# A recurrent attention stage: the written order of its 2208 steps replaced by a rule, with filler matmuls before some waits

## The reference

```python
def step(S, inp):                      # one token, per head of 64
    rt, dt, kt, vt, at, bt = inp
    sa = einsum('bhij,bhj->bhi', S, at)
    S = S * dt[:, :, None, :] + sa[..., None] * bt[:, :, None, :] + vt[..., None] * kt[:, :, None, :]
    y = einsum('bhij,bhj->bhi', S, rt)
...
r, w, k, v, g, a = ...                 # projections of mixtures of x and the token before
y = wkv7(r, w, k, v, -kk, kk * a)      # the scan over 256 tokens
...                                    # group norm, bonus term, gate, output projection
```

## Time and profile before

| | |
|---|---|
| median of 3 executions | 3634.73 us (3626.49 to 3639.4) |
| profiled execution, its own time | 3626.49 us |
| its span, first to last instruction | 3624.7 us |
| busy: PE, DVE, ACT, POOL | 83%, 70%, 50%, 29% of the span |
| mean granted clock of TensorE | 0.893 of full speed |
| stage C | about 1767 to 3189 us of the span |

### The profile page before, as it was taken

One profiled execution on the slowest core, in us unless ns is written; L12 is line 12 of the kernel. 1 busy time (PEld: TensorE's weight loads), 2 busy tenths in 40 slices (PEclk: granted clock), 3 DMA queues, 4 the chain that ended last, 5 costly groups with the idle time before them and its releaser, 6 DMA issues.

```text
span 3624.7 us, 117284 instructions
## 1 busy us (share of the span) xinstructions
PE 3004.9 (83%) x51666; PEld 1961.9 (54%) x51666; DVE 2534.7 (70%) x5294; ACT 1821.0 (50%) x3063; POOL 1048.0 (29%) x1164
## 2 busy tenths in 40 slices
PE   6989999998648988988578888888888887679995
PEld 4555555555325555555245555555555555458773
DVE  3666666665548888988467777877777776457774
ACT  3334444443437888787244544444444552246661
POOL 0332222212431111212232332333333332045552
PEclk8889989989769999999778989989988886689997
DMA  2227999300043344430200000000000000056666
GB/s 75 79 97 290 395 394 327 35 1 1 32 138 125 128 134 138 143 135 21 70 3 4 12 10 11 11 11 11 10 10 10 10 11 14 9 189 227 224 214 180
DMA packets 161676, 356.89 MB, mean 98 GB/s; under 512 B 13821, under 2 KB 98559, under 8 KB 154896
## 3 DMA queue, kind: packets, MB, share of 16 engines
q1 hardware_dynamic: 147088, 323.95, 26.4%
q0 software_dynamic: 14080, 25.45, 2.1%
HBM read 136.33 MB, written 216.67 MB: 97 GB/s over the span
## 4 chain that ended last, share of the span: by engine, by line
PE 45%; issue 19%; DVE 12%; ACT 10%; SPq 9%; DMA 2%; POOL 1%; another core or an unknown queue 0%; DVEq 0%; POOLq 0%; ACTq 0%
PE ps L1551 8%; SPq L2548 8%; PE ps L135 3%; PE ps L137 3%; PE ps L136 3%; PE ps L1616 3%; PE ps L896 2%; ACT t L1035 2%; ACT t L1033 2%; PE ps L903 2%; PE ps L1658 1%; PE ps L875 1%; DVE t L1229 1%; PE ps L1628 1%; ACT t L1037 1%
## 5 line engine op out<-in xcount | busy, mean ns | idle before, releaser
L1551 PE MATMUL ps<-t 128*128 128x512 f32 x608 | 354.1, 697 | 49.3 <-DVE t L2056 11.5
L241 POOL TENSOR_SCALAR_AFFINE_SELECT t<-t 128x512 f32<-128x512 f32 x256 | 168.9, 660 | 666.4 <-ACT t L425 666.4
L485 DVE TENSOR_REDUCE t<-ps 128x2 f32<-128x512 f32 (+1 forms) x512 | 260.7, 551 | 119.9 <-PE ps L304 119.8
L135 PE MATMUL ps<-t 128*128 128x512 f32 (+1 forms) x660 | 279.6, 424 | 57.9 <-DVE t L511 33.4
L425 ACT ACTIVATE t<-ps 128x768 f32<-128x768 f32 x256 | 206.8, 808 | 219.5 <-PE ps L330 219.5
L137 PE MATMUL ps<-t 128*128 128x512 f32 (+1 forms) x660 | 257.5, 390 | 0.0
L136 PE MATMUL ps<-t 128*128 128x512 f32 (+1 forms) x660 | 257.3, 390 | 0.0
L1361 POOL DMA_INDIRECT deltas<-t x92 | 94.4, 1026 | 508.4 <-DVE t L1307 486.2
L2794 POOL DMA_INDIRECT answers<-t x156 | 153.9, 987 | 160.3 <-DVE t L2765 122.4
L1551 PEld LDWEIGHTS ps<-t 128*128 128x128 f32 x608 | 112.6, 210 | 139.3 <-issue 74.9
L135 PEld LDWEIGHTS ps<-t 128*128 128x128 f32 x660 | 127.6, 193 | 108.8 <-DVE t L511 40.6
(11 more groups left out here) (441 smaller groups left out, 8333.8 us busy)
## 6 DMA issues: line engine op xcount, KB each, us to landing
paired<-t SPq DMA_DIRECT2D x14, 8384.0 KB, 60.0
t<-experts SPq DMA_DIRECT2D x39, 1536.0 KB
sorted<-t SPq DMA_DIRECT2D x22, 1950.0 KB, 8.9
t<-in_wP SPq DMA_DIRECT2D x92, 320.5 KB, 3.5
experts<-t SPq DMA_DIRECT2D x8, 1536.0 KB, 6.0
t<-sorted SPq DMA_DIRECT2D x39, 260.0 KB
t<-answers SPq DMA_DIRECT2D x16, 512.0 KB, 6.7
t<-in_wE SPq DMA_DIRECT2D x8, 768.0 KB, 7.6
```

Source lines behind the costliest of these rows:

```text
L135: pe.e.matmul(out, a[0], b[0], start=start, stop=False, skip_group_check=True)
L241: pool.e.affine_select(own, own, [[0, 2], [0, 2], [1, 128]], ALU.is_ge, 0.0, base=0, channel_multiplier=-1).then_inc(*kept(b, j))
L485: m = dve.e.tensor_reduce(nmf[:, z, blk * 16 + 4 * g + i0:blk * 16 + 4 * g + i0 + 2], ps[:, k:k + 2, a0:a1], AX.X, ALU.max, negate=True)
L1551: pe.e.matmul(ps[out, k, :], lhs, rhs, start=True, stop=True).then_inc(*e_pe(u, name))
```

## The change

The table and `HOLD` go. `steps_c` now writes the order by a rule. Unit 0's `E` and the first half's `L` stand alone at the front. Then at most two tiles are in work at a time, the second let in when the first has begun five of its ten steps, and they take turns, one `I` step each. After each `I` step come about one step of each other lane, if the lane's own conditions hold: 0.9 of a step of `E`, 1.05 of `L`, 1.05 of `S`. A unit's `E` starts when the last unit's has ended; its step 21 needs the `L` of the unit before to be done, and its step 9 that unit u-3 has been written back. `S` of a unit starts after the unit's last `I` step. Where the next tile needs an `L` that is not done, `L` steps are written in a row.

`hold` always issues its matmul: the constant `bones` (128x128) by the first n columns of `reset`, float32, into the bank that the following matmuls will overwrite. It stands behind the wait for the bank and ahead of the wait for the data: 128 columns ahead of the turns of `I` step 2, 256 columns ahead of `I` step 9, of the state matmul of six `S` steps, and of `fc`, `rl` and `rk` of `S`.

One wait on DVE changes: step 0 of `E` waits for `xn` of the unit before instead of `k`.

```diff
-UNIT = 138
-AT = {"E": (-243, -236, -219, -216, -208, -198, -188, -183, -179, -170, -162, -151, -147, -138, -136, -133, -132,
...
-HOLD = {"tp": (0, 0, 0, 0), "bd": (0, 0, 0, 0), "s": (0, 0, 0, 0, 0, 0),
-        "fc": 0, "rl": 0, "rk": 0}
+HALFWAY = 5
+STEPS = {"E": 29, "L": 17, "I": 10, "S": 35}
+PACE = {"E": 0.9, "L": 1.05, "S": 1.05}
+WRITTEN = 16
 
 
 def steps_c():
...
-    for _, step in sorted(steps):
-        yield step
...
+    def ready(name):
+        if not lanes[name]:
+            return False
+        u = lanes[name][0][0]
+        if name == "E":
+            return (at["E"] < 9 or u < 3 or ("x", u - 3) in done) and (at["E"] < 21 or ("L", u - 1, 1) in done)
+        if name == "L":
+            k = 4 * (u - 1) + 2 * lanes["L"][0][1] + 1
+            return ("E", u) in done and (k < 0 or begun[k] >= 3)
+        return begun[4 * u + 3] == STEPS["I"]
...
+    for n in range(STEPS["E"]):
+        yield "E", 0, n
+    for n in range(STEPS["L"]):
+        yield "L", 0, 0, n
+    active, k = [], 0
+    while k < 64 or active:
+        if k < 64 and (not active or (len(active) == 1 and begun[active[0]] >= HALFWAY)):
+            while ("L", k // 4, k % 4 // 2) not in done:
+                for name in ("L", "E", "S"):
+                    if ready(name):
+                        yield advance(name)
+                        break
+            active.append(k)
+            k += 1
+        for a in list(active):
+            yield "I", a, begun[a]
+            begun[a] += 1
+            if begun[a] == STEPS["I"]:
+                active.remove(a)
+            for name in lanes:
+                pace[name] = min(pace[name] + PACE[name], 1.0 + PACE[name])
+                while pace[name] >= 1 and ready(name):
+                    yield advance(name)
+                    pace[name] -= 1
+    while lanes["S"]:
+        yield advance("S")
...
         def hold(k, n):
-            if n:
-                pe.e.matmul(ps[:, k, 0:n], w["bones"], w["reset"][:, 0:n], start=True, stop=True, skip_group_check=True)
+
+            pe.e.matmul(ps[:, k, 0:n], w["bones"], w["reset"][:, 0:n], start=True, stop=True, skip_group_check=True)
...
-                hold(b, HOLD["tp"][tile])
+                hold(b, 128)
...
-                hold(b, HOLD["bd"][tile])
+                hold(b, 256)
...
-                    hold(k, HOLD["s"][s])
+                    hold(k, 256)
...
-                hold(k, HOLD["fc"])
+                hold(k, 256)
...
-                hold(k, HOLD["rl"])
+                hold(k, 256)
...
-                hold(k, HOLD["rk"])
+                hold(k, 256)
...
                 if u:
-                    dve.wait_ge(e_dve, u - 1, "k")
+                    dve.wait_ge(e_dve, u - 1, "xn")
```

More of the change, by code:

```diff
@@ L1430 @@
 HS = (16, 8, 4, 2, 1)
-UNIT = 138
-AT = {"E": (-243, -236, -219, -216, -208, -198, -188, -183, -179, -170, -162, -151, -147, -138, -136, -133, -132,
[9 rows of a table removed]
-HOLD = {"tp": (0, 0, 0, 0), "bd": (0, 0, 0, 0), "s": (0, 0, 0, 0, 0, 0),
-        "fc": 0, "rl": 0, "rk": 0}
-def steps_c():
[L1447 to L1454, removed]
-    for _, step in sorted(steps):
-        yield step
+HALFWAY = 5
@@ new lines, with advance @@
+STEPS = {"E": 29, "L": 17, "I": 10, "S": 35}
+PACE = {"E": 0.9, "L": 1.05, "S": 1.05}
+WRITTEN = 16
+def steps_c():
+    lanes = {"E": [(u,) for u in range(1, 16)],
+             "L": [(u, half) for u in range(16) for half in range(2)][1:],
+             "S": [(u,) for u in range(16)]}
+    at = {name: 0 for name in lanes}
+    pace = {name: 0.0 for name in lanes}
+    begun = {k: 0 for k in range(-4, 64)}
+    done = {("E", 0), ("L", 0, 0)}
+    def ready(name):
[8 more added lines that the diff above has]
+        return begun[4 * u + 3] == STEPS["I"]
+    def advance(name):
+        step = (name, *lanes[name][0], at[name])
+        at[name] += 1
+        if name == "S" and at[name] == WRITTEN:
+            done.add(("x", *lanes[name][0]))
+        if at[name] == STEPS[name]:
+            done.add((name, *lanes[name].pop(0)))
+            at[name] = 0
+        return step
+    for n in range(STEPS["E"]):
[24 more added lines that the diff above has]
+        yield advance("S")
```

## The result

The changed kernel takes 3938.93 us, the median of 4 executions (3921.72 to 3956.56), beside 3633.98 us of the kernel before. The ratio is 1.0841, with a 95% interval of 1.0787 to 1.0896. That is 305 us slower, where the prediction said 106 and at most 226.

The account below looks back on a forecast made before the run. PE's own work was taken to bound stage C. Fillers +5.0, clock -2.0 and order +4.0 make +7.0 us a unit, x 16 = +112, forecast 3740 us, range 3650 to 3860.

Parts of the forecast that it names:

- What bounds the kernel: Stage C: PE bound by its own work, 84% busy, 10% gaps of its own, 6% waits for data.
- The fillers: Stage C: filler matmuls cost 6.9 us a unit, 1.9 of it hidden, net +5.0.
- what hides them: Fillers cost nothing where their step would wait anyhow in stage C; taken as 1.9 us a unit.
- The clock: TensorE in stage C: fillers give back clock, -2.0 us a unit, at most 5.4 to 7.2.
- The rival that the clock pays: Stage C: fillers nearly all hidden and hold 2.4 GHz; -3.0 us a unit, 3587 us; chance 0.10.
- The order: Stage C: the rule's order adds PE waits, +4.0 us a unit, between 0 and 8.6.
- the worst filled stretch of the old order: 1850 to 1875 us: PE busy 18.3 us against 21.0 in the mean; upper bound 8.6 a unit.
- Rival 3: Stage C: PE and DVE block each other and the clock gives nothing; +13.6 a unit, 3853 us; chance 0.22.
- The cover: Stage C: PE work between a step and its answer's user; about half of the listed pairs keep enough.
- The DVE wait: `E` step 0 waits for `xn` instead of `k`; both long past on DVE, 0.
- the end: Unit 15's `S` alone at the end of stage C: fillers up to 5 us, clock may return; counted 0.
- pairs that lost their cover: PE work between, table to rule: logits to ranks 13.1 to 6.7 us; `I` 4 to 5, 2.2–5.0 to 0.0–2.9.

Follow-up runs that it names:

- rule_bare: The changed kernel's rule order with no filler at all; median 3925.6 us, ratio 1.0821 against the kernel before.
- table_fill: The kernel before, its table order kept, with the changed kernel's fillers put in; median 3653.9 us, ratio 1.0082 against the kernel before.

## Why the prediction was wrong

**What bounds the kernel.** Right as a reading of the table's order: PE's own work and its "issue" gaps. Two readings under it are off without harm to the forecast: 1040 us are 12.6 units and not 13, and before the first tile the table writes 10 steps of `E` 1 and not 13. What was missed is how little it takes to lose this. DVE has 61 us of work in 80 and TensorE 67; all engines take their steps in place; that TensorE waits for only 4.6 us of data is a property of this one order. Eleven other orders were run, the rule's, two variants of it and eight of the table with steps moved, and without fillers all are 2.7 to 8.2% slower.

**The fillers.** The term was +5.0 net of what hides them. Gross they take 9.4 us in the table and 10.5 under the rule from start to start (11.2 and 12.2 by their records), not 6.9: the estimate in proportion to the columns, from four matmuls in a row, was wrong for single matmuls between others. In the timeline below the filler at 2588.43 has a record of 0.70 us, and 0.54 to the start of what follows, not 0.46. Half of the lone matmul's 1.12 us, which was written down, would have been nearer.

**The clock.** The term was -2.0 with a ceiling of 7.2, and it is about -3.8 in the table and -5.5 under the rule. I discounted it too much: I argued that fillers ahead of data waits do not fill the gaps at "issue", but with these gaps nearly as large as before (6.6 against 8.0 us a unit) the clock rose from 0.90 to 0.95 all the same. Also the fall that I put behind gaps of 1.36 and 1.23 us lies between the two: the granted clock is 1.00 up to 2330.9 us and 0.50 from 2331.0, and the second gap ends at 2332.79. The rule of the Trainium skill that the prediction set beside it ("TensorE: Matmul & The Clock Gate", "Why this matters for your kernels", to keep the engine continuously busy) gave -6. The trace agrees with its direction, and its size lies between the two. The rival that the clock pays was wrong all the same, since the fillers cost more than the clock gives.

**The order.** This is the step that failed: "I take +4.0, a little under the middle of 0 and 8.6". Measured without fillers it is 0.0821 x 3627 / 16 = 18.6 us a unit by the whole time, 20.8 by the period. Two faults are in it. The upper bound was the worst filled stretch of the old order, and it did not bound another order: in `rule_bare` TensorE is idle or waiting for 24.1 us a unit, against 12.8. And the term was waits alone (+13.0 against 4.0), while the clock fell from 0.90 to 0.77 with them and the same work took 9.4 us more. Rival 3 named both, but at 218 us with the same bound.

**The cover.** I compared the PE work between a step and the one that needs its answer with the time that the answer takes with all engines free, and found it enough for about half of the pairs. Why enough is not enough is seen at the ranks, in one unit of the changed kernel. TensorE in order of time: a filler (1584), the logits (1823), two projections, a filler and the ranks (1836).

```profile
2588.43 0.70 PE L1584 MATMUL ps<-t 128*128 128x256 f32 x2
2588.97 0.30 PE L1820 MATMUL ps<-t 128*128 128x32 f32 x2
2589.51 1.06 PE L1823 MATMUL ps<-t 128*128 128x8 f32 x8 [0.25 <-DVE t L2316]
...
2595.98 1.98 PE L1589 MATMUL ps<-t 128*128 128x512 f32 x4
2598.73 0.70 PE L1584 MATMUL ps<-t 128*128 128x256 f32 x2 [0.76 <-DVE t L2094]
2601.27 0.41 PE L1836 MATMUL ps<-t 128*128 128x32 f32 x2 [1.84 <-DVE t L2348]
```

DVE in the same stretch:

```profile
2590.24 1.37 DVE L2185 TENSOR_TENSOR t<-t 128x128 f32<-128x128 f32 x1
2592.80 0.75 DVE L2094 SCALAR_TENSOR_TENSOR t<-ps,t 128x512 f32<-128x512 f32 x1 [1.19 <-PE ps L1589]
2593.47 0.17 DVE L2319 TENSOR_SCALAR t<-t 128x32 f32<-128x32 f32 x1
...
2594.06 0.89 DVE L2323 TENSOR_TENSOR t<-t 128x32 f32<-128x32 f32 x1
...
2597.93 0.74 DVE L2094 SCALAR_TENSOR_TENSOR t<-ps,t 128x512 f32<-128x512 f32 x1
...
2598.79 0.29 DVE L2194 TENSOR_TENSOR t<-t 128x128 f32<-128x128 f32 x1
...
2599.43 1.18 DVE L2342 TENSOR_TENSOR_SCAN t<-t 128x32 f32<-128x32 f32 x1
...
2601.02 0.19 DVE L2348 TENSOR_TENSOR t<-t 128x32 f32<-128x32 f32 x1
```

From the end of the logits, 2590.57, to the ranks at 2601.27 are 10.7 us, against 4.9 with all engines free. TensorE has 8.1 us of work in them (the prediction had 6.7) and is idle for 2.6. Of the 5.8 us more, 2.7 lie in front of the routing operations, where DVE had an `L` step (2185) and a mixture of `E` (2094) to do, which itself waited 1.19 us for a matmul. Another 1.5 us lie in their middle, with a second mixture and three `L` steps. The last 1.7 are the routing operations themselves, which took 6.3 us and not 4.6; most of that is two operations beside GpSimd, of which the last section tells. An answer of one lane waits for the matmul of another, which stood behind a third. The cover of each pair by itself can't show that. That such delays feed each other around the queues is my reading of this stretch and of losses that do not add; no run shows it apart. The filler at 2598.73 also shows why fillers are cheap: its 0.70 us stand where TensorE would have waited anyway, as it did for 1.84 us more.

**What was right.** The DVE wait (0), the end (0), the sign, two of the pairs that lost their cover (the ranks, 25.7 us of waits, and the squaring steps, 45.9), and that the fillers lose more than they win. That their net with the clock, +3.0 a unit, is near the 1.7 to 1.9 measured in the table is luck in its parts. Of the forecasts for the profile, the clock (0.92 to 0.95) would have been that of the table with fillers, 0.95; it fell to 0.85. The waits were to be led by 1551 and 1733, and the squaring steps and the ranks led them; the period was to be 86 to 88 us and is 101.1, past the 93 that the prediction named as a sign that it is wrong.

## What to carry to other kernels

Here all engines walk one list in order, and two of them are 84 and 76% busy. In such a kernel the order was worth more than any single wait in it: the change could not be priced by cover against latency pair by pair, nor bounded by the worst stretch of the order at hand. Moving most steps by about 1 us cost 3 to 6%, and none of eleven other orders was as good, so expect a rewritten order to be slower until it is measured. Besides the answers, look at the banks: the order decides whose bank each matmul inherits. Filler matmuls cost 0.8% or nothing here. Read them by the whole period, never by their busy time, of which most came back as clock, waits and gaps.

## What was not expected of the hardware

Three small DVE operations took 3.5 to 5 times as long as usual beside one of GpSimd. GpSimd in the changed kernel, three instructions of the mixtures (2449), beside DVE's rows above:

```profile
2590.20 1.26 POOL L2449 TENSOR_TENSOR t<-t 128x512 f32<-128x512 f32 x1 [1.49 <-DVE t L2094]
2593.63 1.27 POOL L2449 TENSOR_TENSOR t<-t 128x512 f32<-128x512 f32 x1 [2.17 <-DVE t L2094]
...
2598.76 1.77 POOL L2449 TENSOR_TENSOR t<-t 128x512 f32<-128x512 f32 x1 [3.30 <-DVE t L2094]
```

DVE's 2185 (128x128, median 0.28) took 1.37 us from 2590.24 and ended 0.15 us behind GpSimd's end at 2591.46; the scan 2342 (128x32, median 0.23) took 1.18 us from 2599.43, to 2600.61, with GpSimd's instruction ending at 2600.53; 2323 (128x32, 0.26 in the median) took 0.89 us and ended 0.05 us behind GpSimd's 2594.90. It is one DVE operation each time: 2194 at 2598.79 stands beside the same GpSimd instruction as the scan and took its usual 0.29. The Trainium skill, "GPSIMD Engine Reference", in the table of section 1, says that the two engines share their SBUF interfaces and contend where the DVE instruction has two SBUF inputs; the three long rows agree with it, and 2194, which has two such inputs as well, shows that it does not hold at every moment, as far as GpSimd's spans, which are rough, can tell. In this unit the three are 2.7 us longer than usual together, as much as TensorE's 2.6 us of waiting for the ranks. In the whole they are little: DVE's busy time in the middle of the stage is 805.2 us after and 793.1 before, 0.9 us a unit more. The operation of 2185 is long (over 0.5 us) in 16 of 128 instances after, up to 1.63 us, and in 13 before, up to 0.83.

TensorE's "issue" gaps shrank where it had other waits: 8.0 us a unit in the kernel before, 6.6 with fillers, 5.4 to 6.4 in the slower orders. Their places have a pattern. If the instructions of TensorE (matmuls and weight loads) are counted through the trace, 40 of the 42 such gaps over 0.9 us in the middle of the kernel before come at the same count modulo 256, within two, and they are 63 of the 104.6 us. So do all 41 of `table_fill`, all 24 of the changed kernel and all 26 of `rule_bare`, and none of the 29 waits for data of that length in the kernel before. The long gaps so come with the number of instructions and not with a step of the work. What happens every 256 instructions, and whether fewer instructions would shrink the gaps, no run here shows.
